# Attention scores of a head pair in one burst for both sequences, and VectorE's maxima with them

## The reference, cut to what matters

```python
def attn_layer(x, Wqkv, qs, ksc, Wo):
    q, k, v = ...                      # x @ Wqkv, split in 16 heads of 64
    q = l2norm(q) * qs; k = l2norm(k) * ksc
    q, k = rotary(q), rotary(k)
    sim = einsum('bhwie,bhwje->bhwij', q, k_window) * 8.0
    sim = where(mask, -big, sim)       # i < j or i > j + 32
    out = softmax(sim, -1) @ v_window
    return out.reshape(b, n, 1024) @ Wo
for i in range(6):
    x = attn_layer(shift_tokens(x), ...) + x
    x = ffn_layer(shift_tokens(x), ...) + x
```

## Time and profile before

| | us |
|---|---|
| median of 3 runs (lowest, highest) | 3596.83 (3594.86, 3598.45) |
| the profiled execution | 3596.09 |
| its span, first to last instruction | 3594.3 |
| busy: PE / DVE / ACT / POOL | 3394.7 / 3151.4 / 2999.4 / 2877.3 |
| mean granted TensorE clock | 0.994 of full |

### The profile page before, as it was taken

One profiled execution on the slowest core, in us unless ns is written; L12 is line 12 of the kernel. 1 busy time (PEld: TensorE's weight loads), 2 busy tenths in 40 slices (PEclk: granted clock), 3 DMA queues, 4 the chain that ended last, 5 costly groups with the idle time before them and its releaser, 6 DMA issues.

```text
span 3594.3 us, 92498 instructions
## 1 busy us (share of the span) xinstructions
PE 3394.7 (94%) x29710; PEld 2110.8 (59%) x29710; DVE 3151.4 (88%) x10872; ACT 2999.4 (83%) x8812; POOL 2877.3 (80%) x2383
## 2 busy tenths in 40 slices
PE   7887999999999999999999999999999999999998
PEld 3444656656666666666656666666666656666665
DVE  7998988988988888988988988988988988988986
ACT  6554888888888888888888888888888888888887
POOL 6887887888887888887888887888887888887883
PEclk9998999999999999999999999999999999999999
DMA  5443322333323333322333322333332333332332
GB/s 164 141 133 124 113 99 102 108 115 108 115 101 101 106 112 106 116 103 99 107 115 107 116 102 99 110 116 103 115 106 96 108 118 105 114 106 99 106 103 92
DMA packets 261726, 396.22 MB, mean 110 GB/s; under 512 B 45566, under 2 KB 86588, under 8 KB 261244
## 3 DMA queue, kind: packets, MB, share of 16 engines
q1 hardware_dynamic: 261244, 390.30, 32.4%
HBM read 157.91 MB, written 6.03 MB: 46 GB/s over the span
## 4 chain that ended last, share of the span: by engine, by line
PE 53%; DVE 17%; POOL 14%; issue 7%; ACT 6%; DMA 2%; SPq 1%; DVEq 0%; POOLq 0%; ACTq 0%
PE bank L886 9%; PE bank L875 7%; PE bank L847 6%; PE bank L360 5%; PE bank L362 5%; PE bank L361 5%; DVE ab L1610 4%; PE bank L914 4%; PE bank L829 4%; POOL rot L1359 4%; POOL pr L1345 4%; PE bank L856 4%; DVE wide L1502 3%; PE bank L857 3%; DVE sm L1655 2%
## 5 line engine op out<-in xcount | busy, mean ns | idle before, releaser
L1184 ACT ACTIVATE pr<-sm,nb,rq 128x128 f32<-128x128 f32 (+1 forms) x3072 | 1518.0, 502 | 10.8 <-DVE nb L1661 10.7
L1345 POOL TENSOR_TENSOR pr<-pr,rden 128x640 f32<-128x640 f32 x768 | 966.2, 1258 | 460.1 <-DVE rden L1635 457.7
L1359 POOL TENSOR_TENSOR rot<-ab,swp 128x512 f32<-128x512 f32 x760 | 978.0, 1287 | 74.0 <-DMA swp<-ab 73.4
L1610 DVE TENSOR_TENSOR ab<-bank,ltab 128x1024 f32<-128x1024 f32 x760 | 925.1, 1217 | 80.6 <-PE bank L362 66.7
L1655 DVE CUSTOM_DVE_ANT_0 sm<-bank,mask 128x128 f32<-128x128 f32 (+1 forms) x3072 | 839.4, 328 | 47.5 <-PE bank L847 42.1
L1184 ACT ACTIVATION_READ_ACCUMULATOR pr<-sm,nb,rq 128x1 f32 x3072 | 599.5, 195 | 0.0
L847 PEld LDWEIGHTS bank<-rot 64*64 64x64 f32 x12288 | 288.1, 132 | 436.0 <-issue 364.7
L1365 POOL TENSOR_TENSOR rot<-rot,rkb 128x512 f32<-128x512 f32 x384 | 492.3, 1289 | 64.3 <-DMA rkb<-k_scratch 64.1
L1642 DVE COPY pt<-bank 128x512 f32<-128x512 f32 x768 | 531.3, 692 | 10.2
L875 PE MATMUL bank<-pt,vtok 128*64 128x160 f32 (+1 forms) x6144 | 461.6, 292 | 29.4 <-ACT vtok L1198 29.4
L1172 ACT ACTIVATE sq<-bank 128x512 f32<-128x512 f32 x768 | 452.6, 589 | 43.2 <-DVE ab L1610 19.9
(11 more groups left out here) (213 smaller groups left out, 5743.7 us busy)
## 6 DMA issues: line engine op xcount, KB each, us to landing
swp<-ab SPq DMA_DIRECT2D x1520, 128.0 KB, 2.0
rkb<-k_scratch SPq DMA_DIRECT2D x768, 128.0 KB, 2.9
rot<-c_scratch SPq DMA_DIRECT2D x64, 256.0 KB, 3.3
sq<-c_scratch SPq DMA_DIRECT2D x64, 256.0 KB, 3.3
xs<-xT SPq DMA_DIRECT2D x95, 128.0 KB, 2.3
xs<-xT SPq DMA_DIRECT2D x95, 127.5 KB, 2.4
raw<-Wqkv SPq DMA_DIRECT2D x48, 128.0 KB, 2.7
wo<-Wo SPq DMA_DIRECT2D x6, 512.0 KB, 4.6
```

The costliest lines, as they stand in the source:

```text
L1184: ins = act.activation(pr[:, s % 4, i, t, 0:P + WINDOW * t], sm[:, s % 2, i, cs], ACT.Exp, bias=nb[:, s, t, i:i + 1], scale=head_scale(rq, ...
L1345: ins = pool.tensor_tensor(pr[:, e % 4, :, :, :], pr[:, e % 4, :, :, :], rden[:, e, :, :].rearrange("p t i -> p i t").unsqueeze(3) .to_bro ...
L1359: pool.tensor_tensor(rot[:, PAIRS * (j % 2) + j // 2, :], ab_of(j, 0, lead), swp_of(j, lead), ALU.add).then_inc(qk_rot, 1)
L1610: dve.tensor_tensor(ab_both(j, lead).rearrange("p i (b t) -> p i b t", b=GB), seqs(qk_bank(j, lead)[:, :]).unsqueeze(1).to_broadcast(shape ...
```

## The change

`scores` is called once a head pair, in even steps, and makes the scores of both sequences: 16 matmuls, sequence 0 in columns 0 to 255 and sequence 1 in 256 to 511 of the two banks, keys and score columns at the same place. The first query tile takes 64 keys in place of 96. It waits for `k_norm` as before, and for the biases of the pair before. The maxima `mx` lie in SBUF, with a place for each sequence. In an even step VectorE makes the maxima of this step, those of head 0 of the next, the bias of this step, and the maxima of head 1 of the next; an odd step has no maxima, and its bias stands near the step's head, behind the reciprocals. `outputs` stands right behind `scores`, ahead of the down projection, norm transposes, centring and output projection. `copy_probs` transposes the 32-row strips of two steps in one instruction in even steps, and waits there for the normalised probabilities of the odd one too.

```diff
-SCORE_TILES = [(0, 0, 0), (1, 32, 32), (2, P, P - WINDOW), (3, P + 64, P + 32)]
+SCORE_TILES = [(0, 64), (32, 96), (P - WINDOW, 96), (P + 32, 96)]
+        mx = sb("mx", [P, 2, 2, 2])
-        mx = bank[1][:, UW:UW + 4].rearrange("p (t i) -> p t i", t=2)
@@ TensorE
-                def scores(s):
-                    p, b = s // 2, s % 2
-                    if b == 0:
-                        pe.wait_ge(k_norm, scaled)
-                    pe.wait_ge(sc_bias, used)
-                    c0 = b * SEQ
-                    for half, c, k0 in SCORE_TILES:
+                def scores(p):
+                    pe.wait_ge(k_norm, n8 + (p + 1))
+                    pe.wait_ge(sc_bias, n16 + 2 * p)
+                    for b in range(GB):
+                        c0 = b * SEQ
+                        for m, (k0, count) in enumerate(SCORE_TILES):
...
-                    if cur is not None:
-                        scores(s)
+                    if s % 2 == 0 and cur is not None:
+                        scores(s // 2)
+                    if s % 2 == 0 and s < 6 and prev is not None:
+                        outputs(s, s // 2 + 5, prev)
+                    if s % 2 == 0 and s >= 6 and cur is not None:
+                        outputs(s, s // 2 - 3, cur)
                     bank_work(s, ("dn", "wo", "rqT", "cen"))
...
-                    if s % 2 == 0 and s < 6 and prev is not None:
-                        outputs(s, s // 2 + 5, prev)
-                    if s % 2 == 0 and s >= 6 and cur is not None:
-                        outputs(s, s // 2 - 3, cur)
@@ VectorE
-                    dve.transpose(pt[96:128, e % 4, :, 0, P:P + WINDOW], pr[0:32, e % 4, :, 1, 0:WINDOW])
+                    if e % 2 == 0:
+                        both = slice(e % 4, e % 4 + 2)
+                        dve.wait_ge(p_norm, n16 + (16 * q + e + 2))
+                        dve.transpose(pt[96:128, both, :, 0, P:P + WINDOW], pr[0:32, both, :, 1, 0:WINDOW])
...
-                def maxima(s):
+                def maxima(s, heads):
-                    dve.wait_ge(sc_ps, scores)
+                    dve.wait_ge(sc_ps, n8 + (p + 1))
                     dve.wait_ge(p_exp, used)
...
+                def bias(s):
+                    p, b = s // 2, s % 2
                     dve.wait_ge(sc_max, n16 + (s + 1))
...
+                    if s % 2 and cur is not None:
+                        bias(s)
                     if s < 4 and prev is not None:
                         copy_probs(s + 12, prev)
...
-                    if cur is not None:
-                        maxima(s)
+                    if s % 2 == 0 and cur is not None:
+                        maxima(s, (0, 1))
+                        maxima(s + 1, (0,))
+                        bias(s)
+                        maxima(s + 1, (1,))
```

More of the change, by code:

```diff
@@ L832, in square_sums @@
                     mm.then_inc(sq_part, 1)
-                def scores(s):
-                    p, b = s // 2, s % 2
-                    scaled = (n8 + (p + 1))
-                    used = (n16 + s)
-                    if b == 0:
-                        pe.wait_ge(k_norm, scaled)
-                    pe.wait_ge(sc_bias, used)
-                    c0 = b * SEQ
-                    for half, c, k0 in SCORE_TILES:
[L844 to L848, removed]
+                def scores(p):
[4 more added lines that the diff above has]
+                        for m, (k0, count) in enumerate(SCORE_TILES):
+                            part = slice(64 * (m % 2), 64 * (m % 2) + 64)
+                            for i in range(2):
+                                rows = slice(64 * i, 64 * i + 64)
+                                mm = pe.matmul(bank[i][part, c0 + k0:c0 + k0 + count],
+                                               rot[rows, p, c0 + 64 * m:c0 + 64 * m + 64],
+                                               rot[rows, PAIRS + p, c0 + k0:c0 + k0 + count], start=True, stop=True)
                     mm.then_inc(sc_ps, 1)
@@ L1640, in copy_probs @@
                         dve.wait_ge(o_ps, n8 + (8 * q + e // 2 - 1))
-                    dve.transpose(pt[96:128, e % 4, :, 0, P:P + WINDOW], pr[0:32, e % 4, :, 1, 0:WINDOW])
+                    if e % 2 == 0:
+                        both = slice(e % 4, e % 4 + 2)
+                        dve.wait_ge(p_norm, n16 + (16 * q + e + 2))
+                        dve.transpose(pt[96:128, both, :, 0, P:P + WINDOW], pr[0:32, both, :, 1, 0:WINDOW])
                     dve.tensor_copy(pt[:, e % 4, :, :, 0:P],
                                     bank[2][:, :].rearrange("p (i t c) -> p i t c", i=2, t=2)).then_inc(p_Tsb, 1)
-                def maxima(s):
+                def maxima(s, heads):
                     p, b = s // 2, s % 2
-                    scores = (n16 + (s + 1))
                     used = (n16 + (s - 1 if s >= 2 or prev is not None else 0))
-                    dve.wait_ge(sc_ps, scores)
+                    dve.wait_ge(sc_ps, n8 + (p + 1))
                     dve.wait_ge(p_exp, used)
-                    for i in range(2):
+                    for i in heads:
                         for t in range(2):
                             cs = slice(0, P) if t == 0 else slice(P, UW)
-                            ins = dve.tensor_tensor_reduce(sm[:, s % 2, i, cs], bank[i][:, cs], mask[:, cs],
-                                                           1.0, -3e38, ALU.add, ALU.max, mx[:, t, i:i + 1])
-                    ins.then_inc(sc_max, 1)
+                            keys = slice(b * SEQ, b * SEQ + P) if t == 0 else slice(b * SEQ + P - WINDOW, b * SEQ + SEQ)
+                            ins = dve.tensor_tensor_reduce(sm[:, s % 2, i, cs], bank[i][:, keys], mask[:, cs],
+                                                           1.0, -3e38, ALU.add, ALU.max, mx[:, b, t, i:i + 1])
+                    if 1 in heads:
+                        ins.then_inc(sc_max, 1)
+                def bias(s):
+                    p, b = s // 2, s % 2
                     dve.wait_ge(sc_max, n16 + (s + 1))
@@ L1660, in maxima @@
                         dve.wait_ge(rq_sb, n2 + (s // 8 + 1))
-                    dve.tensor_tensor(nb[:, s, :, :], mx, head_scale(nrq, p, b), ALU.mult).then_inc(sc_bias, 1)
+                    dve.tensor_tensor(nb[:, s, :, :], mx[:, b, :, :], head_scale(nrq, p, b), ALU.mult).then_inc(sc_bias, 1)
                 def clamp(h, q):
```

## The result

The changed kernel takes 3610.35 us, the median of 6 runs (3607.53 to 3611.03), against 3597.64 us of the kernel before: a ratio of 1.0035, 95% interval 1.0022 to 1.0048. It is 13 us slower, 0.26 us a turn. The profiled execution's span is 3608.7 us.

A forecast was written before the change was run, and what follows sets the result against it. Each turn was taken as a TensorE part (40 us) and one set by ScalarE, GpSimd and VectorE (27 us). A gain of 0.4 us over 48 turns, 19 us, gave 3596.1 - 19 = 3577 us, range 3530 to 3628.

The forecast's parts named there:

- TensorE, what the burst saves: Scores as one burst per head pair: 0.82 us instead of 0.98, with entry 0.2 us saved per pair, 1.6 a turn.
- VectorE, what it saves: Bias waits, joint transpose and maxima on VectorE: net 0.64 us saved per pair, 5.1 us a turn.
- I take no change: Maxima written to SBUF instead of PSUM: no change in time, bounds 0.03 us each way.
- Step 7: TensorE's transposes wait for VectorE's copy of the same step; TensorE loses 0.45 us of its 1.2.
- the walk: Pass through steps 7, 8 and 10 of a turn, charging each wait in full; it leaves 0.2 us a turn.
- Step 8: Centring stands behind outputs and a longer burst; ScalarE's square is 0.3 us late, absorbed by a 0.34 us gap.
- Step 10: Maxima of step 11 wait some 0.4 us for step 9's exponentials; ScalarE's square starts 0.5 us late.
- Rival C: Slower: loop of exponentials, odd step's maxima, bias, copy, products, square limits ScalarE's part; 3620 to 3654 us, chance 0.27.
- Bias(even): Sign of being wrong: this bias, 0.5 us later in its step, holds up exponentials in the TensorE part too.
- Bias(13): At the head of step 13, no longer behind 2.5 us of work; ScalarE reaches gelu about 0.15 us earlier.
- forecast A: TensorE's gain mostly spent, 0.2 to 0.8 us a turn left: 3558 to 3587 us, value 3577, chance 0.40.
- rival B: TensorE part passes its gain on in full, 1.0 to 1.7 us a turn: 3515 to 3548 us, chance 0.18.

The follow-up runs named there:

- e7: Kernel before with the burst alone: transposes one by one, outputs in their old place, maxima in each step and in PSUM; 3592.38 us, ratio 0.9975.
- e2: Changed kernel with the maxima back in PSUM, in score columns already read, order of work unchanged; 3593.36 us, ratio 0.9990 to the kernel before.
- e1: Kernel before with one thing changed, the maxima in SBUF instead of PSUM; 3667.64 us, ratio 1.0199.
- e9: Changed kernel with maxima and bias made in each step, maxima left in SBUF; 3604.57 us, ratio 1.0015 to the kernel before.
- e4: Changed kernel with maxima and bias made in each step and the maxima in PSUM; 3558.85 us, ratio 0.9893 to the kernel before.
- e14: Changed kernel with a third buffer for the masked scores, maxima left in SBUF; 3588.95 us, ratio 0.9967 to the kernel before.
- e3: Changed kernel with all outputs back behind the output projection; 3615.28 us, ratio 1.0053 to the kernel before.

## Why the prediction was wrong, by its own steps

**TensorE, what the burst saves.** Right as work: the burst is 0.82 us on the chain, as summed. The burst alone (e7) makes TensorE's busy time 0.2 us a pair shorter. In the changed kernel it fell by 102.7 us, 0.27 a pair, the outputs' move with it; 0.2 for the burst and the move's 0.2 to 0.4 a turn make up to 0.25.

**VectorE, what it saves.** The joint transpose takes 304 ns for 239, as summed (0.07 more). The maxima were sized too high: a read of the accumulator into SBUF takes 82 ns for 140, and from the first of the four maxima to the last read it is 0.90 us (1726.76 to 1727.66) for 1.02. By the read's own length, 0.058 us, that is outside the bound of 0.03 an instruction, and the prediction had named it as a sign of being wrong; by the spacing it is at the bound. It is on the good side. VectorE's busy time, forecast 60 to 150 us down, is 112.7 down, but by other terms: the transposes' records give the 66 that was forecast, the maxima and their reads some 260 more, and the biases take 149 back (records overlap, so the sum is larger than the fall). That the total came out in the range is luck.

**"I take no change" for the maxima in SBUF.** This is the first of the two steps that failed. The prediction took the maxima's move to SBUF as free. It weighed the length of the instruction in the earlier trace rows and not what it reads. The bias reads two tensors; one lay in PSUM, and both lie in SBUF now. GpSimd is busy 80% of the span, so many a bias meets it, and its mean went from 162 ns to 355. e2 against the changed kernel prices it at 16 us here, e1 at 71 and e9 against e4 at 44 where each bias follows its maxima. None of the rivals held it. The Trainium skill states it: "SBUF — State Buffer", SBUF: two separate sides, says that VectorE and GpSimd share a pair of ports, and that of an instruction of VectorE with two SBUF inputs and a GpSimd operation that reads SBUF the one that starts first has the pair for its whole length while the other waits. The traces agree for a bias that starts second: in the changed kernel and in e1 all 249 and 389 long biases end within 0.03 us of the end of a GpSimd operation, and with one input in PSUM (before, e2) none takes over 206 ns. Five biases of the changed kernel that start inside a GpSimd scaling of 772 ns (`gg<-gg,lv`) are short all the same, and ten are held by it; what makes the difference is open. Whether a bias that starts first delays GpSimd was not looked at.

**Step 7, 0.45 us lost before the transposes.** Not in this turn: VectorE's copy is ready when TensorE comes. Over the run that wait shows 13 times in steps 6 and 7, with 11.5 us. The same wait in steps 11 and 13 was not in the walk, and comes in every turn: 1.14 and 1.66 us in this one, and 127.5 of the run's 142.5 us (the kernel before has 8.2). With the third buffer 93.4 are left of it (e14).

**Step 8, centring 0.3 us late.** Wrong in sign. (Its own terms add up to 1712.60, not 1712.65.) ScalarE's square of it starts at 1720.34, 35.7 us into the turn, against 35.9 in the earlier trace rows. ScalarE does wait there for 1.02 us, but after exponentials that end 1.3 us earlier in the turn than before.

**Step 10, a wait of 0.4 us.** This is the second step that failed: the right wait, sized a quarter of what it is. It is 1.79 us in this turn and 1.8 on average in step 10, and another 0.4 in step 12, in all 113.3 us over the run, 2.4 a turn. The slip was to let VectorE start the maxima of step 10 when it did before, at 1720.51, 44.0 us into the turn. But step 9 has no maxima any more; VectorE arrives 42.1 us into it, 1.9 earlier, while ScalarE's exponentials end only 0.6 earlier (44.7 for 45.3), and nearly all of the rest becomes waiting. The third buffer shows what the wait is worth at the end: 24 us in the changed kernel, 31 with maxima in PSUM. Rival C had this mechanism. Its loop from the exponentials' end to the next square, 3.4 us, is 3.2 here (1729.40 to 1732.58), its wait was too small, and its range lay above what came. The two waits that were to be read first, of the maxima for exponentials and of the transposes for the copy, are 256 us together, and over 150 was the prediction's sign for C.

**Bias(even), the last sign of being wrong.** ScalarE waits for biases for 158.3 us, 152 us of it in steps 0 to 5, in TensorE's part, as the sign has it. But e3 has only 18.7 us of that wait, with ScalarE waiting for the outputs in its place, and is not faster, so nothing shows that this wait moved the end.

**Bias(13) and the sum.** ScalarE's table load for the gelu starts at 1743.93, 59.3 us into the turn as before (1735.81), where 0.15 us were to be gained. The walk left a gain of 0.2 us a turn, the forecast took 0.4, and the result is a loss of 0.26. Port (16) and wait (24) together are 40 us by the runs that remove one each, and 47 by the one that removes both. Without them the rest of the change is worth 0.95%, 34 us, which lies between forecast A (19) and rival B (48 and more). That does not bear out B: of the 75 us that the burst takes off TensorE, 9 reach the end alone (e7), and it needs the joint transpose and the outputs' move beside it for more. Each of the two losses was enough to turn the sign: without the wait the changed kernel is at 0.9967, without the port at 0.9990. The 3610 us lie inside the stated range of 3530 to 3628 only because the range took in the near half of C; the forecast was a gain.

## What to carry to other kernels

When an operand moves from PSUM to SBUF, list for each reader what else it reads, and which engine shares that path; the reader's own duration in the old trace says nothing about it. When work is pulled ahead of its old place, look up who has to have left the buffer it writes, and count the wait from the new, earlier arrival, not from the old start. One more buffer for the masked scores (2.3 KB a partition) bought back nearly all that pulling the maxima ahead had cost with maxima in PSUM, and nothing beyond. The simplest form was as fast: burst, early outputs and joint transpose, with the maxima in PSUM and left in their steps, 3558 to 3559 us, 1.1 to 1.2% under the kernel before.

## What the runs showed that was not expected

VectorE's read of an accumulator takes 82 ns into SBUF and 140 into PSUM, and the maxima that it ends start 0.03 us closer together. A four-element instruction cost 71 us of 3597 in e1. It stands between VectorE's maxima and both ScalarE and TensorE. Its mean of 433 ns for 162 adds 208 us to its records; the cheaper reads of the maxima hide part of that, and VectorE's busy time rises by 76.
